# Logits by half tiles, low weights by an accumulating DMA, and a new order of VectorE's split parts in an audio tower layer

## What is computed

```python
def _L0_ffn_ref(x, ...):
    xt = jnp.transpose(x, (0, 2, 1))
    rc = jax.nn.gelu(conv1d_same(xt, rc_w1, rc_b1), approximate=False)   # 3 taps, 128 -> 128
    rc = conv1d_same(rc, rc_w2, rc_b2)                                   # 3 taps, 128 -> 10
    logits = jnp.transpose(rc, (0, 2, 1)).reshape(-1, E)
    vals, idx = jax.lax.top_k(logits, 2)
    gv = jax.nn.softmax(vals, axis=-1)
    ...
    h = jax.nn.elu(jnp.einsum('nd,edh->enh', x2, e_w1) + e_b1[:, None, :])
    eo = jnp.einsum('enh,ehd->end', h, e_w2) + e_b2[:, None, :]
    y = jnp.einsum('end,ne->nd', eo, gates).reshape(B, T, d)
    sh = jax.nn.silu(conv1d_same(xt, sh_w1, sh_b1))                      # 9 taps, 128 -> 512
    sh = conv1d_same(sh, sh_w2, sh_b2)                                   # 1 tap, 512 -> 128
    z = residual + y + jnp.transpose(sh, (0, 2, 1))
    return layer_norm(z) * ln_g + ln_b
```

## Time and profile before

| | us |
|---|---|
| median of 3 executions | 159.66 |
| lowest and highest | 159.06, 160.29 |
| the profiled execution | 159.7 |
| its span | 157.8 |
| TensorE, VectorE busy | 145.6 (92%), 129.4 (82%) |
| ScalarE, GpSimd busy | 75.7 (48%), 87.7 (56%) |

### The profile page before, as it was taken

How to read it: one execution, slowest core, us unless ns; L and a number is a source line. 1 busy time by engine, 2 the same in 40 slices (tenths; PEclk the granted TensorE clock), 3 DMA queues, 4 the chain that set the end, 5 groups by cost and what they waited for, 6 DMA issues and landing times.

```text
span 157.8 us, 3057 instructions
## 1 busy us (share of the span) xinstructions
PE 145.6 (92%) x998; PEld 131.6 (83%) x998; DVE 129.4 (82%) x356; ACT 75.7 (48%) x201; POOL 87.7 (56%) x79
## 2 busy tenths in 40 slices
PE   7799879999998999999999988999999999999950
PEld 2599669999985747899999958999999999979830
DVE  0087999999998989879977765999999999895871
ACT  2223965201018769971043424677777777741030
POOL 3063899999999984004777720056464454470230
PEclk9999999999999999999999999999999999999999
DMA  5999999992980000000399229999899985004304
GB/s 150 262 395 412 295 201 277 209 123 50 199 150 2 2 0 4 0 0 0 64 334 324 93 73 287 391 386 360 308 320 283 355 296 198 34 33 130 124 0 116
DMA packets 19619, 28.57 MB, mean 181 GB/s; under 512 B 4838, under 2 KB 14182, under 8 KB 19604
## 3 DMA queue, kind: packets, MB, share of 16 engines
q1 hardware_dynamic: 16984, 21.69, 44.5%
q0 software_dynamic: 1696, 5.52, 14.6%
q10 hardware_dynamic: 924, 1.17, 2.8%
HBM read 19.94 MB, written 5.28 MB: 160 GB/s over the span
## 4 chain that ended last, share of the span: by engine, by line
PE 64%; POOL 13%; DVE 7%; DMA 7%; issue 4%; ACT 2%; SPq 0%; DVEq 0%; POOLq 0%
PE psum L629 14%; PE psum L746 13%; PE psum L760 12%; POOL xs_rows L501 9%; DMA xT_s<-xT 4%; PE psum L858 4%; POOL prod L351 4%; PE psum L718 3%; PE psum L537 3%; PE psum L733 2%; PE psum L560 2%; DVE stats L1153 2%; DMA xs_rows<-xT_s,slot 1%; DMA xb<-xs_rows 1%; PE psum L549 1%
## 5 line engine op out<-in xcount | busy, mean ns | idle before, releaser
L511 POOL DMA_INDIRECT ys_rows<-yb,xid x22 | 21.1, 961 | 24.9 <-ACT yb L1109 24.9
L1099 ACT ACTIVATE wu<-psum,wring 128x128 f32<-128x128 f32 x92 | 26.1, 373 | 11.2 <-PE psum L746 11.2
L1408 DVE SCALAR_TENSOR_TENSOR tb<-psum,wring,wu 128x128 f32<-128x128 f32 x92 | 25.9, 344 | 0.8
L760 PE MATMUL psum<-wring,tb 128*128 128x128 f32 x184 | 24.6, 276 | 0.2 <-DVE tb L1408 0.2
L746 PE MATMUL psum<-xTb,wring 128*128 128x128 f32 x184 | 24.3, 275 | 0.0
L501 POOL DMA_INDIRECT xs_rows<-xT_s,slot x14 | 14.4, 1027 | 16.1 <-DVE slot L1340 12.1
L760 PEld LDWEIGHTS psum<-wring,tb 128*128 128x128 f32 x184 | 22.4, 192 | 1.1 <-DVE tb L1408 1.0
L629 PE MATMUL psum<-prod,ident_s 128*128 128x196 f32 (+1 forms) x120 | 21.6, 341 | 1.1 <-POOL prod L351 1.1
L746 PEld LDWEIGHTS psum<-xTb,wring 128*128 128x128 f32 x184 | 22.4, 192 | 0.0
L629 PEld LDWEIGHTS psum<-prod,ident_s 128*128 128x128 f32 x120 | 21.1, 190 | 1.2 <-issue 1.2
L363 POOL TENSOR_TENSOR prod<-es,vt 128x3136 f32<-128x3136 f32 x3 | 19.4, 6479 | 0.2 <-ACT es L979 0.2
(11 more groups left out here) (185 smaller groups left out, 276.8 us busy)
## 6 DMA issues: line engine op xcount, KB each, us to landing
wring<-wexp SPq DMA_DIRECT2D x23, 514.0 KB, 4.9
wu<-raw POOLq DMA_DIRECT2D x2, 1536.0 KB, 11.6
raw<-wsh SPq DMA_DIRECT2D x2, 768.0 KB, 9.1
xs_rows<-zero_s SPq DMA_DIRECT2D x1, 1472.0 KB, 16.2
ys_rows<-zero_s SPq DMA_DIRECT2D x1, 896.0 KB, 17.7
xT_s<-xT SPq DMA_DIRECT2D x2, 384.0 KB, 6.0
wu<-wsh SPq DMA_DIRECT2D x1, 768.0 KB, 7.3
xb<-xs_rows SPq DMA_DIRECT2D x1, 585.0 KB, 6.2
```

The costliest lines, as they stand in the source:

```text
L511: pool.indirect_dma_start(ys_dram, bass.IndirectOffsetOnAxis(ap=xid[:, j:j + 1], axis=0), yb[:, j % NY, :], None)\
L760: ins = mm(y_ps(j), tb[:, j % NTT, c, :], wring[:, j % NR, W2 + c * P:W2 + (c + 1) * P], start=(c == 0), stop=(c == HC - 1))
L1099: ins = A(eb[:, j % NEB, c, :], ps[U_BANKS[j % NU]][:, c * P:(c + 1) * P], ACT.Exp, bias=wring[:, j % NR, B1 + c:B1 + c + 1])
L1408: ins = V.scalar_tensor_tensor(tb[:, j % NTT, c, :], ps[U_BANKS[j % NU]][:, c * P:(c + 1) * P], wring[:, j % NR, B1 + c:B1 + c + 1], eb[:, ...
```

## The change

It does five things.

1. The logits are computed by halves of a slot, with 64 stationary columns instead of 128: 18 products instead of 9. Nine of them, those that need only the first half's gelus, stand right behind the convolution, the others behind `with_high(0, 1)`. The filler matmul between is gone. The logits now lie in bank 5 instead of 4.
2. The low part of weight set 2 is no longer a VectorE subtraction. ScalarE's high part is made negative; GpSimd issues an accumulating DMA that adds it to `wu12[:, 1]`, and ScalarE copies the difference, negative as well, to `wu12_l[:, 1]`. The signs in `shared_sums` are turned for that.
3. On VectorE the three forms stand ahead of the two first low parts. The third low part is cut in two: one half behind the picks, one behind the gates. `keep_rows(1)` moves behind the slots.
4. On ScalarE the first high part moves behind the first half's gelus, and the first sum behind the gate weights.
5. TensorE's products of c = 0 and 1 stand in another order; before `with_high(1, 1)` there is a wait for `keep_rows(1)`.

```diff
+L_BANK = 5
...
             pool.tensor_tensor(wu12_l[:, 0], wu12[:, 0], wu_h[:, 1], ALU.subtract).then_inc(S("wu1_l"), 1)
+            pool.wait_ge(S("wu_h_done"), 4)
+            pool.dma_start(wu12[:, 1], wu_h[:, 2].bitcast(F32), accum_op=ALU.add).then_inc(S("wu2_rest"), 16)
...
+            def logits(hf, i):
+                a = (i * (KRC + 1) + KRC - 1) * E
+                taps = ps[L_BANK][hf * B:(hf + 1) * B, a:a + KRC * KRC * E].rearrange("p (t x) -> p t x", x=KRC * E)[:, :, 0:E]
+                return mm(taps, rT9[:, i, hf, :], wrc2_s[:], start=True, stop=True)
+            pe.wait_ge(S("bias_set"), 1)
+            pe.wait_ge(S("zeroed"), 2)
+            pe.wait_ge(S("gelu_done"), 2)
+            for i in range(NT + 1):
+                logits(0, i)
+            logits(1, 0)
             with_high(0, 1)
-            keep_going(1, M_BANK[0][3])
+            pe.wait_ge(S("gelu_done"), 4)
+            logits(0, NT + 1)
+            for i in range(1, NT + 2):
+                ins = logits(1, i)
+            ins.then_inc(S("L_mm"), 1)
             with_low(0, 1)
-            pe.wait_ge(S("gelu_done"), 4)
-            pe.wait_ge(S("bias_set"), 1)
-            for i in range(NT + 2):
-                ...
-                ins = mm(taps, rT9[:, i].rearrange("p h b -> p (h b)"), wrc2_s[:], start=True, stop=True)
-            ins.then_inc(S("L_mm"), 1)
             low_weights(0, 1)
             with_high(0, 2)
             with_low(0, 2)
-            for m in (0, 3):
-                with_high(0, m)
-            low_weights(0, 0, False)
+            with_high(0, 0)
...
             ins.then_inc(S("count_mm"), 1)
-            low_weights(0, 3, False)
+            with_high(0, 3)
+            for m in (0, 3):
+                low_weights(0, m, False)
+            low_weights(0, 2)
+            with_high(1, 2)
+            with_high(1, 0)
+            low_weights(1, 0, False)
+            pe.wait_ge(S("h2_done"), len(LN_GROUPS))
             with_high(1, 1)
             with_low(1, 1)
             low_weights(1, 1)
-            with_high(1, 2)
             with_low(1, 2)
-            with_high(1, 0)
-            low_weights(1, 0, False)
             for m in (0, 3):
                 with_low(0, m, True)
-            low_weights(0, 2)
             with_low(1, 0, True)
...
-            A(wu_h[:, 2], wu12[:, 1], ACT.Copy).then_inc(S("wu_h_done"), 1)
+            A(wu_h[:, 2], wu12[:, 1], ACT.Copy, scale=-1.0).then_inc(S("wu_h_done"), 1)
...
-            act.wait_ge(S("h2_done"), len(LN_GROUPS))
+            act.wait_ge(S("h2_done"), len(LN_GROUPS) - 1)
...
-            high_part(0)
             for hf in range(2):
...
                 if hf == 0:
                     gelu(rT9[:, 0, 1, :], ps[6][:, HW - B:HW])
+                    high_part(0)
...
-            first_sum(0)
+            act.wait_ge(S("wu2_rest"), 16)
+            A(wu12_l[:, 1], wu12[:, 1], ACT.Copy, scale=-1.0).then_inc(S("wu2_l"), 1)
             act.wait_ge(S("dm_done"), 1)
...
+            first_sum(0)
             first_sum(1)
...
-            for n, k in enumerate((2, 0, 1)):
+            for k in (2, 0):
                 keep_rows(k).then_inc(S("h2_done"), 1)
...
-            form(0)
-            form(1)
-            low_part(0)
-            form(2)
-            low_part(1)
+            for n in range(3):
+                form(n)
+            for n in range(2):
+                low_part(n).then_inc(S("dsf_l"), 1)
...
             V.tensor_tensor(dm[:], top8[:, :, 1], top8[:, :, 0], ALU.subtract).then_inc(S("dm_done"), 1)
+            low_part(2, slice(outer.start, middle)).then_inc(S("dsf_l_half"), 1)
...
-            low_part(2)
-            dve.wait_ge(S("wu_h_done"), 4)
-            V.scalar_tensor_tensor(wu12_l[:, 1], wu12[:, 1], 1.0, wu_h[:, 2], ALU.mult, ALU.subtract).then_inc(S("wu2_l"), 1)
+            keep_rows(1).then_inc(S("h2_done"), 1)
...
             V.tensor_tensor(gates[:, :, 0:E], gsum[:, 0], gsum[:, 1], ALU.add).then_inc(S("gates_done"), 1)
+            low_part(2, slice(middle, outer.stop)).then_inc(S("dsf_l"), 1)
```

More of the change, by code:

```diff
@@ L1291, in form, with low_part @@
                 V.tensor_tensor(dsf[:, sl], xp[:, a:a + w], xp[:, b:b + w], c).then_inc(S("dsf_form"), 1)
-            def low_part(n):
+            def low_part(n, part=None):
                 dve.wait_ge(S("dsf_h"), n + 1)
-                sl = dsf_range(M_ORDER[n])
-                V.scalar_tensor_tensor(dsf_l[:, sl], dsf[:, sl], 1.0, dsf_h[:, sl], ALU.mult, ALU.subtract).then_inc(S("dsf_l"), 1)
+                sl = part or dsf_range(M_ORDER[n])
+                return V.scalar_tensor_tensor(dsf_l[:, sl], dsf[:, sl], 1.0, dsf_h[:, sl], ALU.mult, ALU.subtract)
             dve.wait_ge(S("wu_l_pool"), 4)
@@ L1301, in _ @@
             dve.wait_ge(S("xp_done"), len(LN_GROUPS))
-            form(0)
-            form(1)
-            low_part(0)
-            form(2)
-            low_part(1)
+            for n in range(3):
+                form(n)
+            for n in range(2):
+                low_part(n).then_inc(S("dsf_l"), 1)
+            outer = dsf_range(M_ORDER[2])
+            middle = (outer.start + outer.stop) // 2
             iota = rows_s[:, R_IOTA, :]
@@ L1353, in shared_sums @@
                 even, odd = halves(rr[c % 2])[:, 0], halves(rr[c % 2])[:, 1]
[L1354 to L1355 removed]
+                V.scalar_tensor_tensor(even, sums(c, 2), -0.25, c1[c % 2], ALU.mult, ALU.add)
+                V.scalar_tensor_tensor(odd, sums(c, 2), 0.25, c1[c % 2], ALU.mult, ALU.add).then_inc(S("uv_done"), 1)
                 dve.wait_ge(S("uv_done"), c + 1)
```

6 lines of the change are left out of this document (1 added, 5 removed).

## The result

Over 22 runs each, taken in turn, the changed kernel takes 158.77 us and the kernel before 159.95. The ratio is 0.9938 with a 95% interval of 0.9922 to 0.9954: 1.0 us faster, between 0.7 and 1.2. That is within the 1% that the prediction counts as no change to the whole. The profiled execution has a span of 157.0 us instead of 157.8.

A forecast was written before the change was run, and what follows sets the result against it. Routing to the gathered rows was taken to bound the blocks' start, 1.20 us behind TensorE's products. Routing 0.65 us earlier moves the start from 95.17 to 94.5, giving 159.1 us from 159.7; range 158.3 to 160.8.

The forecast's parts named there:

- the forecast's own way: Start of the expert blocks: routing 0.65 us earlier, gathered rows (xb) arrive last at 94.5; 159.1 us, chance 0.44.
- the two paths: Ahead of the blocks: routing to the gathered rows, 94.5, and TensorE's product stream, 94.3, ending 0.2 us apart.
- Logits by halves: TensorE's router logits: 36 instructions of 64 columns at 53 ns each, 1.93 us in all, nothing added.
- the rival: Half-slot logits cost full loads: 107 ns an instruction, +1.93 us on the logits, 160.3 us; chance 0.24.
- both claims on the reduction: VectorE's first reduction waits for the logits and VectorE's second low part; forecast 0.60 us earlier, set by the low part.
- The waits that go: Routing on TensorE and VectorE: logits end 1.2 us earlier, reduction 0.60, half of what TensorE gives; over 0.65 earlier.
- Waiting before the count: TensorE is through with five products behind the logits at 68.7, then waits about 0.9 us for the picks.
- Fewer collisions: GpSimd's first two scatters lose 0.95 us, xb at 93.6, TensorE's 94.3 decides: 158.9 us; rival's chance 0.20.
- The ceiling: TensorE's product stream before the blocks: last matmul from 93.3 to 94.3 instead of 93.97, 0.4 us later, limiting the gain.
- The late sum: GpSimd's accumulating DMA held out, landing at 72.6, delaying gates and scatters: 162.0 us; rival's chance 0.06.
- the cover: Gates done at 70.9, first scatter wants them by about 71.7: 0.8 us, so the DMA may land at 69.5.

The follow-up runs named there:

- halves_together: Changed kernel with both halves of the logits in a row and with_high(0,1) behind them; ratio to the kernel before 0.9938.
- full_logits: Changed kernel with the logits again as nine full-slot products (128 columns), all behind with_high(0,1); ratio to the kernel before 0.9965.
- early_logits: Kernel before with the logits ahead of with_low(0,1) instead of behind it, and no filler matmul; ratio to the kernel before 1.0036.
- two_sbuf: Changed kernel plus two unused 128x1024 VectorE instructions behind the slots, both inputs in SBUF; ratio to the kernel before 1.0017.
- one_psum: Changed kernel plus two unused 128x1024 VectorE instructions behind the slots, first input in PSUM; ratio to the kernel before 1.0027.
- one_more: Changed kernel with with_high(0,3) moved ahead of the count; ratio to the kernel before 0.9922.
- after_copy_first: Changed kernel with ScalarE's copy of the blocks ahead of the last tanh and VectorE's last shared piece behind the third block's; ratio to before 0.9950.
- later_sum: Changed kernel with two more 768 KB DMAs ahead of the accumulating one on GpSimd's queue; ratio to the kernel before 0.9985.

## Why the prediction was right, and where it was not

**The size.** 0.6 us were forecast, 1.0 measured (0.7 to 1.2), 0.75 in the traces at the first expert product. The time, 158.77, lies in the range. That it is near the forecast says little for the forecast's own way, in which the gathered rows come last: the two paths were forecast to end 0.2 us apart, so either of them as the last gives nearly the same time. Two misses also worked against each other. The rows gained more at the first two scatters than was forecast, and TensorE's stream, with the detour behind it, took part of that away. The routing part, step by step, was very near: reduction forecast at 66.66 and found at 66.67, picks at 69.44 and 69.45, `over` at 70.17 and 70.06, DMA landing at 67.1 and 66.8, copy to 70.2 and 70.1, gates at 70.9 and 70.7, TensorE's last matmul from 93.3 and 93.25.

**Logits by halves.** 58 ns an instruction, near the 53 taken and far from the 107 of the rival, though a load of 64 columns shows a mean of 137 ns and one of 77 columns 145. The duration of a load is no guide to its pitch; the doubt drawn from the earlier trace rows was misplaced. With 58 ns the logits end at 66.5, hardly ahead of the low part: both claims on the reduction had met, as halves_together and full_logits show from either side. The logits were to end 1.2 us earlier. They end 6.53 us behind the convolution's first matmul instead of 7.30 (66.43 against 67.15 in the traces' own times), 0.8 us earlier. What is missing stands under the next point but one.

**The waits that go.** That half of what TensorE gives is lost to the low part holds. The prediction did not see how the gain hangs on TensorE's list: it wrote that the products "led straight into the count" and did not ask whether the count was late by them. It was: the picks were done 0.36 us ahead of it (70.04 and 70.40), and with one product more in early_logits it came another 0.27 us later.

**Waiting before the count.** 0.9 us forecast, 0.3 found. TensorE was ready at 69.3 and not at 68.7: 0.14 us from a convolution that ended at 63.57, 0.16 from 36 instructions at 58 ns, 0.20 from the product between the halves, which took 0.75 (64.62 to 65.37), and 0.10 from the first one behind them (66.43 to 67.09), where 0.555 each was taken. The count itself came as forecast, since the picks set it.

**Fewer collisions.** The step that failed is the weighing of this rival at 0.20. It is the case: the first scatter took 0.54 us less, the second 0.23, and two_sbuf against one_psum shows the cause for 0.51. The argument against it misread a row: the scatter at 80.49 does not lie under a VectorE instruction at its start, it starts 0.02 us before one (80.51), and the scatter at 85.33 in the changed kernel, which does start under such a piece, took 1.12 us. The forecast's own way, xb last at 94.5, did not happen; the rows were there by 94.09, and that rival's bound, TensorE's stream, was the right one, if by little in this execution. That rival had the rows at 93.6. Counted from the convolution, they gained 0.82 us at the first scatter and 0.75 at the first two, and lost 0.42 again: 0.23 under the other scatters, of it 0.15 at the one from 85.33, and 0.19 between the last scatter and the load. An estimate from these numbers: with the collisions still there the rows would have come 0.75 us later, at 34.94 from the convolution, and the first expert product, 0.96 behind them as in the kernel before, at 35.90 instead of 35.53. So about half of the 0.75 us found there hangs on the collisions.

**The ceiling.** The transposes started at 94.11, 0.2 us ahead of the 94.3 of this bound, as the end of the last matmuls ahead of them was taken from a modelled duration (1.02) where the pitch is 0.86. And it was not the whole bound: behind the stream stand VectorE's last sum, ScalarE's tanh and the copy of the blocks, 0.25 us more, a wait that the trace of before did not show because rows came too late for it. one_more and after_copy_first show it by taking it away.

**The late sum** did not happen: the issue took 0.94 us with a form of VectorE's running, and was not held out. Its threshold was forecast at 69.5. In later_sum the copy was 2.04 us late and the scatter 1.29, so the cover is 0.75 us (0.8 forecast) and the threshold 68.63 + 0.75 = 69.4. Of the 1.29 us at the scatter 0.97 arrived at the first transpose and 0.76 at the first expert product, as there the wait of 0.25 us for the detour was gone.

## What to carry to other kernels

When a result is handed back and forth between engines, look at each hand-over for the second claim: what the receiving engine is doing just then, and how long the list of the other one is before it looks again. Bringing the sender forward is worth only the gap to that second claim, and may cost when it lengthens the other list. And before a stage is said to start with its data, follow the queue of each engine that has to touch them, not the first one alone: a wait of 1.2 us hid a chain of product, sum, tanh and copy that ended 0.25 us behind TensorE's own work.

## What the runs showed of the hardware

A scatter issued by GpSimd took 0.51 us longer (1.61 against 1.10) when VectorE ran instructions with both inputs in SBUF than when one input lay in PSUM, at the same duration of 2.35 us on VectorE (for two), and in six cases the excess was 0.01 to 0.05 us less than the time until VectorE's next instruction. Under a short piece of 192 elements it was still 0.15 us. Stationary loads of 64 columns come at a pitch of 58 ns against 107 for 128, though their single durations read 137 and 192 ns. A further 768 KB on GpSimd's queue put the landing of the transfer behind it off by 1.8 us, two by 3.9 (6.9 us from the convolution's first matmul in the changed kernel, 8.7 and 10.8 in the two runs).
